# 72 of layer 1's 256 strips multiplied during layer 0 of a four-layer graph network

## What is computed

```python
x = _layernorm(x + L0(x, adj, W0))       # adj @ (gamma*XW), adj @ (gamma-1), row sums of adj; then per-row tanh/artanh maps
x = _layernorm(x + L1(x, adj, W, b))     # below
x = _layernorm(x + L2(x, adj, ...))      # softmax(sim*adj) mixed with the degree-scaled adj, times x
x = _layernorm(x + L3(x, adj, ...))      # adj @ x, then a GRU cell

def L1(x, adj, W, b):
    a_hat = adj + eye(n)
    d = where(isinf(deg ** -0.5), 0, deg ** -0.5)    # deg = row sums of a_hat
    return ((a_hat * d[:, None] * d[None, :]) @ x) @ W.T + b
```

## Time and profile before

| | us |
|---|---|
| three timed runs | 1427.14, 1430.31, 1425.74 (median 1427.14) |
| the profiled execution | 1429.81, span 1428.0 from first to last instruction |
| layer 0, first multiply to layer 1's first | 38.7 to 419.5 |
| layer 1 | 419.5 to about 638 |
| layer 2, then layer 3 | to 1161.7, to the end |

### The profile page before, as it was taken

How to read it: one execution, slowest core, us unless ns; L and a number is a source line. 1 busy time by engine, 2 the same in 40 slices (tenths; PEclk the granted TensorE clock), 3 DMA queues, 4 the chain that set the end, 5 groups by cost and what they waited for, 6 DMA issues and landing times.

```text
span 1428.0 us, 21041 instructions
## 1 busy us (share of the span) xinstructions
PE 1315.2 (92%) x7640; PEld 1017.7 (71%) x7640; DVE 1076.5 (75%) x1936; ACT 1072.9 (75%) x1376; POOL 577.5 (40%) x441
## 2 busy tenths in 40 slices
PE   5999999999988989996899999999998879999995
PEld 5999999999986767772566666666665658666763
DVE  6855555555668989985788887888878869777874
ACT  6887888888776767757888878888797547667663
POOL 4312221323364442423477767677776640000010
PEclk9999999999999999998999999999999989999998
DMA  9999999999957868883578778787786749877750
GB/s 308 398 378 365 351 351 362 360 335 354 341 193 296 307 253 342 325 353 123 211 278 302 272 268 312 264 298 281 265 318 189 276 168 411 332 263 266 296 184 22
DMA packets 114808, 413.08 MB, mean 289 GB/s; under 512 B 10000, under 2 KB 23568, under 8 KB 90128
## 3 DMA queue, kind: packets, MB, share of 16 engines
q1 hardware_dynamic: 106256, 407.54, 77.7%
q10 hardware_dynamic: 8448, 4.20, 1.0%
HBM read 340.40 MB, written 71.30 MB: 288 GB/s over the span
## 4 chain that ended last, share of the span: by engine, by line
PE 50%; DVE 19%; ACT 18%; issue 7%; POOL 4%; DMA 2%; POOLq 0%; ACTq 0%; DVEq 0%; SPq 0%
DVE part_l L1321 7%; PE strip_b L576 5%; PE acc L521 4%; PE acc L512 4%; PE acc L513 4%; PE acc L493 3%; PE mid L493 3%; ACT arena L732 3%; PE acc L593 3%; ACT arena L814 3%; DVE part_l L1200 3%; ACT part_h L787 2%; PE acc L590 2%; PE acc L591 2%; PE strip_b L473 2%
## 5 line engine op out<-in xcount | busy, mean ns | idle before, releaser
L1321 DVE TENSOR_TENSOR part_l<-arena,part_h 128x1024 fp32r<-128x1024 f32 x256 | 327.2, 1314 | 59.0 <-ACT part_h L787 57.6
L1034 POOL TENSOR_TENSOR part_l<-arena,part_h 128x512 fp32r<-128x512 f32 x237 | 304.0, 1296 | 156.8 <-ACT part_h L825 156.6
L787 ACT ACTIVATE part_h<-arena 128x1024 fp32r<-128x1024 f32 x256 | 265.3, 1055 | 125.3 <-PE acc L521 110.9
L1200 DVE TENSOR_TENSOR part_l<-arena,part_h 128x1024 fp32r<-128x1024 f32 x128 | 160.9, 1266 | 120.4 <-ACT part_h L739 119.8
L825 ACT ACTIVATE part_h<-arena 128x512 fp32r<-128x512 f32 x256 | 157.6, 623 | 95.2 <-DVE arena L1395 89.8
L512 PE MATMUL acc<-part_h,Y 128*128 128x512 f32 x512 | 220.4, 430 | 3.2 <-ACT part_h L787 1.9
L513 PE MATMUL acc<-part_h,Y 128*128 128x512 f32 x512 | 204.0, 398 | 0.0
L1002 POOL TENSOR_TENSOR sc<-sc,power 128x4 f32<-128x4 f32 x32 | 49.3, 1542 | 329.5 <-DVE sc L1226 329.5
L576 PEld LDWEIGHTS strip_b<-ident,arena 128*128 128x128 f32 x1024 | 127.2, 142 | 68.8 <-DVE arena L1395 19.3
L521 PE MATMUL acc<-part_l,Y 128*128 128x512 f32 x512 | 164.7, 403 | 10.6 <-DVE part_l L1321 10.2
L576 PE MATMUL strip_b<-ident,arena 128*128 128x128 f32 x1024 | 157.5, 277 | 15.4 <-DVE arena L1395 10.3
(11 more groups left out here) (257 smaller groups left out, 2776.5 us busy)
## 6 DMA issues: line engine op xcount, KB each, us to landing
arena<-adj_t SPq DMA_DIRECT2D x128, 1024.0 KB, 4.6
arena<-in_adj SPq DMA_DIRECT2D x64, 1024.0 KB, 8.6
adj_t<-arena SPq DMA_DIRECT2D x64, 1024.0 KB, 7.1
arena<-in_adj SPq DMA_DIRECT2D x128, 512.0 KB, 6.2
part_h<-adj_t SPq DMA_DIRECT2D x64, 512.0 KB, 5.5
part_l<-adj_t SPq DMA_DIRECT2D x64, 512.0 KB, 5.0
scratch<-v ACTq DMA_DIRECT2D x8, 256.0 KB, 10.6
arena<-scratch SPq DMA_DIRECT2D x8, 256.0 KB, 5.9
```

Source lines behind the costliest of these rows:

```text
L787: act.activation(flat(part_h[:, slot:slot + 2, :]), turned_pair(n), ACT.Copy).then_inc(high_done, 1)
L1034: pool.tensor_tensor(part_l[:, b % 4, :], mixed[b % G_SLOTS], part_h[:, b % 4, :].bitcast(F32), ALU.subtract).then_inc(low_done, 1)
L1200: dve.tensor_tensor(flat(part_l[:, slot:slot + 2, :]), full_pair(n), flat(part_h[:, slot:slot + 2, :]).bitcast(F32), ALU.subtract).then_in ...
L1321: dve.tensor_tensor(flat(part_l[:, slot:slot + 2, :]), turned_pair(n), flat(part_h[:, slot:slot + 2, :]).bitcast(F32), ALU.subtract).then_ ...
```

## The change

1. **Layer 0 multiplies some strips for layer 1 too.** `FUSED` = 4 and `fused(s) = min(4, max(s-1, 0))`: in slab s the groups 0 to fused(s)-1 are also multiplied with layer 1's input, whose rows for slab g are ready by slab g+2. That is 0, 0, 1, 2, 3, 4, 4, 4 groups of 4 strips, 72 strips. `Y` becomes two planes of `inputs`, and a third plane holds the high part of layer 1's input, so that the matmul of `part_h` has 390 columns, that of `part_l` 260, and a third one (`part_h` with the low part) has 128; the sums lie in columns 260 to 387 of the same banks.
2. **The order of groups.** From slab 2 on the groups of layer 0 come as 0, 4, 1, 5, 2, 6, 3, 7.
3. **Partial sums.** After slabs 2 to 7 ACT copies the new columns out in two halves (`read_partial`), SP stores them to DRAM (256 KB, `put_partial`) and brings them back in layer 1 (`load_partial`); POOL adds them to the identity's share (`add_partial`).
4. **Layer 1 is shorter.** `TURNS1` leaves the 36 pairs out: 92 steps. `ROWS_FROM[1]` becomes 30, 40, 46, 58, 68, 76, 84, 92.
5. **Reading the banks of layer 0.** Two reductions on DVE add the halves while reading (`sums_of`), in place of four copies and two additions.
6. **Memory.** The product with W0 (`mx`) takes the place of `x_nat`, and x is loaded a second time in slab 1 (`load_x`, 2 x 1 MB). The unit vectors are made in `v_of` and moved by a DMA from ACT's queue (hook 15, 256 KB a slab) into the freed third plane; `x_bias` of slab s waits for the DMA of slab s-2.
7. `y_scale` and the split of layer 1's first four groups move into slabs 1 to 4 (`y1_parts`, on ACT and POOL).

The core of the diff:

```diff
+FUSED = 4
+def fused(s):
+    return min(FUSED, max(s - 1, 0))
+GROUPS0 = [list(range(GROUPS)) if s < 2 else [0, 4, 1, 5, 2, 6, 3, 7] for s in range(SLABS)]
+INPUTS1 = [0, 4, 1, 5, 2, 3] + [SLABS - 2, SLABS - 1]
+TURNS1 = [(s, 2 * g + h) for s in range(2) for g in INPUTS1[:-1] for h in range(2)] \
+    + [(s, 2 * INPUTS1[-1] + h) for s in range(2) for h in range(2)] \
+    + [(s, m) for s in range(2, SLABS) for m in range(2 * fused(s), PAIRS)]
+ROWS_FROM = {1: [TURNS1.index((s, PAIRS - 1)) + (9 if s == 1 else 1) for s in range(SLABS)],
...
+                if g == s - 2 and g < FUSED and m % 2 == 0:
+                    pe.wait_ge(y1_low_done, g + 1)
...
+                        sums = acc0[q][:, 0:3 * LO].rearrange("p (h w) -> p h w", w=LO)
+                        if both:
+                            if start:
+                                pe.matmul(sums, h, planes[:, :, j, :], start=True, stop=False)
+                            pe.matmul(sums[:, 0:3:2, :], low, planes[:, 0:3:2, j, :], start=False, stop=False)
+                            if not start:
+                                pe.matmul(sums, h, planes[:, :, j, :], start=False, stop=False)
+                            last = pe.matmul(sums[:, 2, 0:D], h, y1_low[:, j, :], start=False, stop=False)
...
+            def load_x(h):
+                blocks = slice(NB // 2 * h, NB // 2 * (h + 1))
+                sp.wait_ge(y_ready, 4 * h + 4)
+                sp.dma_start(x_nat[:, blocks, :], x.rearrange("(b p) d -> p b d", p=P)[:, blocks, :]).then_inc(x_again[h], 16)
...
+            def load_partial(s):
+                sp.wait_ge(partial_out[s % 2], partials_at(s))
+                sp.wait_ge(row[s % 2], row_done(1, s - 2, "ln_out"))
+                sp.dma_start(t_of[s % 2], partials[s].rearrange("p (q d) -> p q d", d=D)).then_inc(partial_in[s % 2], 16)
...
+            def read_partial(s):
+                act.wait_ge(product, slab_product(0, s))
+                act.activation(partial(s)[:, 2:4, :], both0(1)[:, :, 2 * LO:2 * LO + D], ACT.Copy).then_inc(partial_half, 1)
+                act.wait_ge(sums_half, s + 1)
+                act.activation(partial(s)[:, 0:2, :], both0(0)[:, :, 2 * LO:2 * LO + D], ACT.Copy).then_inc(partial_read, 1)
...
+                if k == 15:
+                    act.wait_ge(row[s % 2], row_done(1, s, "unit_low"))
+                    act.dma_start(halves_of[:, s, :, :].bitcast(F32), unit_new[s % 2]).then_inc(units_in[s % 2], 16)
...
+            def add_partial(s):
+                pool.wait_ge(eye_scaled, s - 1)
+                pool.wait_ge(partial_in[s % 2], partials_at(s))
+                pool.tensor_tensor(by_block(eye[s % 2]), by_block(eye[s % 2]), t_of[s % 2], ALU.add).then_inc(eye_in, 1)
...
                 if k == 0:
                     before("x_bias")
+                    if s >= 2:
+                        pool.wait_ge(units_in[par], 16 * (s // 2))
...
             def read_acc0(s):
                 dve.wait_ge(product, slab_product(0, s))
-                dve.tensor_copy(nat[:, 2, :], acc0[2][:, 0:YW])
-                dve.tensor_copy(nat[:, 3, :], acc0[3][:, 0:YW]).then_inc(acc_read, 1)
+                for n in range(2):
+                    parts = both0(n)[:, :, 0:2 * LO].rearrange("p q (h w) -> p q w h", w=LO)
+                    if n == 1 and s >= 2:
+                        dve.wait_ge(partial_half, s - 1)
+                    dve.tensor_reduce(sums_of[s % 2][:, 2 * n:2 * n + 2, :], parts, AX.X, ALU.add
+                                      ).then_inc([sums_half, acc_read][n], 1)
```

More of the change, by code:

```diff
@@ L22 @@
 PAIRS = NB // 2
-YW = 2 * D + 4
 LO = D + 2
@@ L648, in _ @@
                 multiply0(n)
-            for n in range(TURNS_ALL):
+            for n in range(STEPS1):
                 for k, s in hooks(1, n):
@@ L910, in _ @@
                     y_high(3, (m - 6) % NB // 4)
-            for n in range(TURNS_ALL):
+            for n in range(STEPS3):
                 if n < PAIRS // 2:
@@ L1084, in _ @@
                         eye_share(s)
+                    if n == ROWS_FROM[1][s] - 2 and s >= 2:
+                        add_partial(s)
             for n in range(STEPS2):
```

327 lines of the change are left out of this document (205 added, 122 removed).

## The result

The changed kernel takes 1440.2 us (median of 5 runs, 1436.7 to 1442.6); the kernel before took 1427.6 beside it (median of 5, 1425.7 to 1430.3). The ratio is 1.0080, with a 95% interval of 1.0063 to 1.0096: slower by 11.4 us (9 to 14). The profiled execution took 1440.22 us with a span of 1438.0, against a span of 1428.0 before, so the two traces differ by 10.0 us. In what follows lengths are compared between profiled executions, and times by their ratio to the kernel before, at 14.3 us for each 1%.

What follows compares the result with a forecast made beforehand. PE was taken to set the pace, with DVE also full in layer 1. Layer 0 +39.1, layer 1 -39.4 and its end +5.0 gave +4.7 on 1429.81, or 1434.5; 2.7 lower at the median, 1432 us (1424 to 1441; 8-in-10 1408 to 1450).

Steps and rivals of the forecast that it cites:

- fused columns: Layer 0, PE: the added matmul columns cost 1.42 us a fused step, +51 us over 72 strips.
- reading the banks, 7 boundaries: Layer 0: PE waits for DVE's two reductions, about 0.57 us longer at each of 7 slab boundaries, +4.0 us.
- y's parts: Layer 0: scaling and splitting moved onto ACT and POOL lie beside PE, no cost; without cover 3 us a slab.
- second load of x: Layer 0, slab 1: reloading 2 MB delays stores that free `full`; +1.5 us, between 0 and 5.6.
- waits that are swallowed: Layer 0, slabs 3 to 7: longer PE steps cover existing waits, -17.4 us, from -8 to -25.
- The bounds of +35 and +78: Layer 0's added columns: +35 us if only columns count, +78 if each matmul pays 0.05 us on top.
- The estimate of +44 us: Layer 0's added columns costed by the Trainium skill's figures: 383 ns for three matmuls, +44 us.
- The collisions at distance 8: Layer 1: row chains of neighbouring slabs 8 steps apart stall PE, 4.3 us for each of slabs 6 and 7.
- slab 3's stall: Layer 1, slab 3: the wait for POOL's `x_bias` shrinks from 6.95 to 3.3 us, plus 1.2 for DVE.
- DVE's bound: Layer 1's short slabs: DVE needs 16.4 us for 8 steps, PE 14.5; slab 4 loses 2.0, slab 5 2.5.
- The end of layer 1: After layer 1's last product, slab 7's row chain up to the first exponential comes later, +5.0 us.
- the rival at 10.6: Layer 1: unit vectors' DMA lands in 10.6 us, not 4.5, delaying `x_bias` of four slabs; +20, 1452 us, chance 0.12.

Runs made afterwards that it cites:

- no_columns: The changed kernel with layer 0 leaving out the 72 strips of layer 1 (except first strips of slabs 2 to 7), all else kept: 1411.5 us, ratio 0.9868.
- y1_later: The changed kernel with y's parts of groups 1 to 3 made in the third pair of the slab after: 1435.5 us, ratio 1.0028.
- bias_first: The changed kernel with a slab's `x_bias` issued on POOL ahead of the previous slab's unit rows where both share a step: 1434.2 us, ratio 1.0033.
- partial_earlier: The changed kernel with POOL's `add_partial` issued two steps earlier in layer 1, ahead of that step's row operations: 1436.2 us, ratio 1.0050.
- three_orders: The changed kernel with all three edits of y1_later, partial_earlier and bias_first: 1422.9 us, ratio 0.9957.

## Why the prediction was right, and where its size was off

The side was right and the mechanism too: an even exchange on PE, spoiled by rows that collide. 1432 was forecast and 1440.2 came, just inside the forecast's own range of 1424 to 1441; between the traces +4.7 was forecast and +10.0 came, so the size was less than half. That it isn't further off is partly luck: layers 0 and 1 came 9.7 us longer than forecast (3.3 and 6.4), and 3.8 came back in layers 2 and 3, where no work was changed. In layer 0 errors cancelled as well. Its sum by terms, each measured one from steps of the traces:

```
                                            forecast   measured
fused columns                                 +51       +50.4
reading the banks, 7 boundaries                +4.0      +3.6
y's parts                                       0        +8.5
second load of x (step 7 of slab 1)            +1.5      +1.3
first step of slab 0, at the lower clock        0        +2.0
what is left: waits that are swallowed        -17.4     -23.4
```

**The fused columns: right.** Forecast 1.42 us a step and 4.1 us a fused step; measured 4.14 to 4.18 against 2.75, so 1.40, and 36 of them 50.4 against 51. A block's three matmuls, in PE's list of slab 5, take 0.42 from one low part to the next (297.99 to 298.41; forecast 0.41):

```profile
297.99 0.34 PE L590 MATMUL acc<-inputs,part_l 128*128 128x260 f32 x1
298.17 0.34 PE L592 MATMUL acc<-inputs,part_h 128*128 128x390 f32 x1
298.35 0.22 PE L593 MATMUL acc<-inputs,part_h 128*128 128x128 f32 x1
298.41 0.33 PE L590 MATMUL mid<-inputs,part_l 128*128 128x260 f32 x1
```

The bounds of +35 and +78 were not reached.

The estimate of +44 us from the figures of the Trainium skill (TensorE: Matmul & The Clock Gate, sections LDWEIGHTS and Back-to-back issue gap) was further off than the one from rows. It set 383 ns by the page against the pair's 0.23 us by rows; with the page's figures on both sides (107 + 111 = 218 ns for the pair) the estimate is +47.5, and the trace has 50.4.

**Swallowed waits: right in kind, 6 us too small.** Against the kernel before they are 23.4, within the 8 to 25 of the forecast. Slabs 5 and 6 were to take 56.5 and took 56.0, and slab 7 swallowed 8.7 against 8.1; but slabs 2 and 3, which the forecast gave 0 and 0.45, swallowed 1.3 and 2.9. That they are swallowed, and not the columns free, was argued in the prediction and is shown by no_columns.

**Reading the banks: right.** The last step of a slab is 3.56 where ACT is on time, 3.04 before: 0.52 against 0.57 forecast. The first step of slab 0 took 4.77 us in this execution, at a granted clock of 0.54, and 2.76 or 2.77 in six traces of the variants above; that is the execution and not the change.

**y's parts: the step that failed in layer 0.** The prediction put ACT's and POOL's scaling and splitting beside PE, "with ACT 7.9 and POOL 35 us idle a slab". Idle time in a slab is no cover for a wait in an engine's queue: ACT stood 4 times for POOL, 15.6 us, with PE's copies queued behind it. y1_later moves three of the four and slabs 2 to 4 become 6.3 us shorter; in slab 1 the fourth still costs 1.8, and 0.4 in the last step. That makes 8.5, or 2.1 a slab, for a term that the sum had at nothing; the 3 a slab that the prediction named for the case without cover were nearer.

**The second load of x: the right size in this trace.** The loads landed after 12 us. Slab 1's step 7 took 4.41 in this execution, 3.50 to 4.31 in five of the other traces with this load and 3.14 or 3.15 in six, so the 1.3 us of this trace are often nothing.

**Layer 1: 6.4 us too hopeful, by slabs 3 and 4.** By slab, measured and forecast: slabs 0 and 1 +0.9 and 0; slab 2 22.94, as forecast; slab 3 28.88 and 24.5; slab 4 22.44 and 19.2; slab 5 15.75 and 17.0; slab 6 18.96 and 18.8; slab 7 17.9 and 19.0. Slabs 3 and 4 are 7.6 over, and slabs 5 and 7 give 2.3 back. The collisions at distance 8 were right: forecast 18.8 with PE idle for `x_bias`, and bias_first takes them away. Two steps failed. First, slab 3's stall was to shrink from 6.95 to 3.3, because I followed only the chain on POOL; that chain did go, and ACT's read of the bank, now directly behind `normed` and 2.9 us later in the slab than before, took over and kept the step at 8.39. That is read from the order and the times (the read and L641 are 0.10 or 0.11 us apart in four traces); no run turned the two round on ACT. I had not asked what is late next, on another engine. Second, `add_partial` was costed as 0.9 us of contention for DVE and not as a wait. It queues behind unit vectors, and L628 waited 8.1 us for it in layer 1; partial_earlier removes this. DVE's bound, which I gave 2.0 and 2.5 us in slabs 4 and 5, lay hidden under that wait: DVE is busy 17.34 of 22.44 in slab 4, and 17.47 of 17.64 in three_orders, where the wait is gone. So the bound exists, at 17.6 and not at the 19.2 forecast.

**The end of layer 1: right, 4.97 against 5.0**, with two errors that cancel. L641 started 4.4 us after ACT began the read, 0.7 before: 3.7 later, against 4.5 forecast; what follows to the first exponential is 1.2 longer, against 0.5. The transfer that I listed as a rival does bind there: `x_bias` of slab 7 waited for it, 0.80 us; it landed 6.6 us after its issue. The eight landings were 2.3 to 6.6 us, median 3.7, so the value of 4.5 stands and the rival at 10.6 doesn't.

**Layers 2 and 3** are 3.2 and 0.6 us shorter, for no work of theirs. In the thirteen other traces layer 2 takes 501.6 to 504.8, so it is the kernel before's 506.7 that stands out: the kernel before with one number changed in layer 1 has 504.8. What makes the rest I leave open.

## What to carry over

When work is moved between two stages that are both at TensorE, expect nothing from the move itself; cost the orders around it, since here they were worth 17.6 us and the exchange of ten steps more or less was worth nothing that shows. Idle time of an engine hides an added operation only if the operation's own input is ready when its turn comes; else name what is queued behind it. Where a stall has a chain, look at all engines for the second latest before you write the stall off: slab 3's kept its length with another cause.

## What the runs showed of the hardware that I had not expected

POOL's product with a broadcast column, 128x512, takes 1.04 us in some turns and up to 5.36 in others, in steps of about 1.1 us. The steps go by what DVE makes beside it: 1.03 or 1.04 with none of DVE's low parts (and 1.32 once, where one was just ending), 3.09 with two, 4.22 with three, 5.36 with four (a fifth began 0.9 us before its end and took 1.99 itself). This holds in all 32 turns of the traces before, after, y1_later and three_orders. In the changed kernel's layer 0 it took 3.09 in six of seven turns:

```profile
391.99 1.04 POOL L1097 TENSOR_TENSOR turned<-arena,dcol 128x512 f32<-128x512 f32 x1
394.28 3.09 POOL L1097 TENSOR_TENSOR turned<-arena,dcol 128x512 f32<-128x512 f32 x1 [1.25 <-DVE arena L1401]
...
394.11 2.36 DVE L1363 TENSOR_TENSOR part_l<-arena,part_h 128x1024 fp32r<-128x1024 f32 x2
```

A low part has two inputs in SBUF. DVE's scaling L1233, with one, ran beside the product at 358.10 in the kernel before, and the product took 1.04. Wherever low parts lengthen it, it ends 2.12 us after the start of the last of them. By these numbers 2.05 us of each of ACT's four waits for y's parts are this collision (an estimate, 3.09 - 1.04). The times on POOL are rough, and no run moved the two apart on purpose.

A stall costs more than its idle time. In slab 3 of the changed kernel's layer 1 the clock over the stretch is 0.88 and in slab 6 of three_orders 0.83; and after 4 us without work the matmuls of 512 columns start 0.42 to 0.43 us apart (593.94, 594.37, 594.79 in slab 5's first step) in place of 0.23; the granted clock there is 0.50, the lower of its two levels, 1.2 GHz; such steps take up to 2.71 us in place of 1.39. It doesn't follow every wait: after the 3.22 us before 634.81 the clock stayed at 1.00. Where y1_later takes the waits out of slab 3 of layer 0, the clock is 1.00 for 0.97 and the step after the wait is back from 3.95 to 2.74.
